# Making TensorE's 128-column products as four products on 32-column tiles, in a fused decoder layer

## The reference, cut to what matters

```python
x = x + mixer(_layernorm(x))        # projection 512 -> 2576, causal conv of 4 taps, silu, scan over 512 tokens,
                                    # 16 heads x 16 states; y -> 1024 channels, gated by silu(z), -> 512
x = x + attention(_layernorm(x), ctx, ctx)   # q is the normed x (32 heads of 16), k = v = ctx (8 kv heads)
x = x + moe(_layernorm(x))          # 16 experts, top 2, plus a shared expert; F = 256

scores  = jnp.einsum('bkgsd,bktd->bkgst', qh, kh) / 4.0      # 512 x 512 for each of 32 heads, each batch
weights = jax.nn.softmax(scores, axis=-1)
out     = jnp.einsum('bkgst,bktd->bkgsd', weights, vh)
```

## Time and profile before

| | |
|---|---|
| median of 3 runs | 1274.8 us (1274.4 to 1276.44) |
| the profiled execution | 1273.91 us |
| its span, first to last instruction | 1272.1 us |
| mean granted TensorE clock | 0.988 of 2.4 GHz |
| PE busy | 1212.4 us (95% of the span), 5041 matmul records |
| PEld / DVE / ACT / POOL busy | 40% / 53% / 38% / 25% |
| attention slot 0 begins | 191.4 us |

### The profile page before, as it was taken

How to read it: one execution, slowest core, us unless ns; L and a number is a source line. 1 busy time by engine, 2 the same in 40 slices (tenths; PEclk the granted TensorE clock), 3 DMA queues, 4 the chain that set the end, 5 groups by cost and what they waited for, 6 DMA issues and landing times. The chain is left out here.

```text
span 1272.1 us, 14831 instructions
## 1 busy us (share of the span) xinstructions
PE 1212.4 (95%) x5041; PEld 508.7 (40%) x5046; DVE 673.8 (53%) x1116; ACT 486.2 (38%) x685; POOL 314.8 (25%) x459
## 2 busy tenths in 40 slices
PE   6999999999999999999999999999988999999995
PEld 3444434343434434344433333333334444444442
DVE  3833595656687565668574776767447222222220
ACT  3311324534555353555453455555520222222221
POOL 6012310311321220221032121111103344444443
PEclk9989999999999999999999999999998999999998
DMA  8320774104374101263500255000037465678640
GB/s 197 98 76 21 202 145 111 34 5 113 83 144 84 55 22 37 72 134 80 106 9 14 87 97 76 35 2 1 34 120 273 89 171 109 163 214 226 165 88 17
DMA packets 112963, 121.14 MB, mean 95 GB/s; under 512 B 18897, under 2 KB 78417, under 8 KB 112769
## 3 DMA queue, kind: packets, MB, share of 16 engines
q1 hardware_dynamic: 101936, 99.11, 30.1%
q0 software_dynamic: 10528, 21.12, 8.4%
q10 hardware_dynamic: 432, 0.08, 0.0%
HBM read 94.63 MB, written 28.97 MB: 97 GB/s over the span
## 5 line engine op out<-in xcount | busy, mean ns | idle before, releaser
L670 DVE TENSOR_REDUCE mx<-ps_m 128x2 f32<-128x1024 f32 x256 | 313.2, 1223 | 244.1 <-PE ps_m L1141 242.1
L839 ACT ACTIVATE prob<-ps_s 128x1024 f32<-128x1024 f32 x256 | 261.9, 1023 | 335.2 <-PE ps_s L1124 335.2
L1066 PE MATMUL acc<-xnT,wring 128*128 128x512 f32 x560 | 279.8, 599 | 2.8 <-DVE xz L588 2.0
L1773 PE MATMUL ps_gu<-ring,xgT 128*128 x376 | 176.7, 593 | 0.9 <-issue 0.9
L1141 PE MATMUL ps_m<-k_stack,q_stack 96*128 96x512 bf16 x512 | 153.0, 380 | 6.6 <-DVE mx L670 5.9
L1124 PE MATMUL ps_s<-q_stack,k_stack 99*128 99x512 bf16 x512 | 153.9, 382 | 5.5 <-ACT prob L839 5.3
L1502 DVE COPY xgT<-ps_x 128x512 f32<-128x512 f32 x47 | 32.5, 691 | 204.5 <-PE ps_x L1745 200.0
L1154 PE MATMUL ps_o<-prob,values 128*32 128x512 f32 x1024 | 138.3, 604 | 0.0
L1066 PEld LDWEIGHTS acc<-xnT,wring 128*128 128x128 f32 x560 | 104.5, 192 | 70.3 <-issue 36.8
L1453 POOL DMA_INDIRECT out<-y,dest x47 | 74.4, 1584 | 156.3 <-DMA out<-y,dest 105.8
L1124 PEld LDWEIGHTS ps_s<-q_stack,k_stack 99*128 99x128 bf16 x512 | 35.5, 97 | 183.2 <-issue 131.6
(11 more groups left out here) (271 smaller groups left out, 1203.5 us busy)
## 6 DMA issues: line engine op xcount, KB each, us to landing
ring<-in_w_experts SPq DMA_DIRECT2D x96, 256.0 KB
wring<-in_w_in SPq DMA_DIRECT2D x80, 256.0 KB, 3.6
q_stack<-part_rows SPq DMA_DIRECT2D x96, 128.0 KB, 4.8
wring<-in_w_out SPq DMA_DIRECT2D x32, 256.0 KB, 3.0
part_rows<-part SPq DMA_DIRECT2D x20, 384.0 KB, 3.8
xt<-in_x SPq DMA_DIRECT2D x16, 256.0 KB, 4.1
k_stack<-part_rows SPq DMA_DIRECT2D x48, 64.0 KB, 4.2
xn_rows<-xt SPq DMA_DIRECT2D x3, 1024.0 KB, 4.2
```

The source lines that it names most:

```text
L670: nc.vector.tensor_reduce(mx[:, n % G, 2 * u:2 * u + 2], ps_m[:, :, :], AX.X, ALU.max).then_inc(s_max, 1)
L839: nc.scalar.activation(prob[:, slot % PROB, :, :], ps_s[:, :, :], ACT.Exp, scale=SCALE).then_inc(s_exp, 1)
L1066: ins = nc.tensor.matmul(bank(b, n), weights, xnT[:, k, :], start=(k == 0), stop=(k == KD - 1))
L1773: ins = nc.tensor.matmul(ps_gu[p][:, :], xgT[:, p, k * P:(k + 1) * P], weights(own)[:, k * 2 * F:(k + 1) * 2 * F], start=(k == 0), stop=(k ...
```

## The change

A switch `tiled[0]` is off in the slots below 0 and on from slot 0 to the end of the stream phase. While it is on, each product that went through the whole array is issued as four: the stationary operand is cut into four slices of 32 columns, each slice goes to its column tile, all four read the same moving operand, and each writes its 32 partitions of the same PSUM bank. The semaphore increment sits on the fourth. The waits stay ahead of the first.

The fp32 transposes (L978, L985, L992, L1029, L1169, L1184) stay as they were, whole-array operations. `transpose_max` (bf16, 12 columns) and the products that already were on column tiles are not edited.

```diff
             taken = []
+            tiled = [False]
+
+            def product(dst, stationary, moving, start, stop):
+
+                if not tiled[0]:
+                    return nc.tensor.matmul(dst, stationary, moving, start=start, stop=stop)
+                for c in range(0, P, 32):
+                    ins = nc.tensor.matmul(dst[c:c + 32, :], stationary[:, c:c + 32], moving, start=start, stop=stop,
+                                           tile_position=(0, c))
+                return ins
...
-                    ins = nc.tensor.matmul(ps_t[:, :], state_sum[:, k, :], csb[:, k, :],
-                                           start=(k == 0), stop=(k == NS - 1))
+                    ins = product(ps_t[:, :], state_sum[:, k, :], csb[:, k, :], start=(k == 0), stop=(k == NS - 1))
...
-                ins = nc.tensor.matmul(bank(b, n), weights, xnT[:, k, :], start=(k == 0), stop=(k == KD - 1))
+                ins = product(bank(b, n), weights, xnT[:, k, :], start=(k == 0), stop=(k == KD - 1))
...
-                    ins = nc.tensor.matmul(ps_s[:, i, :], k_stack[:, g, t * P:(t + 1) * P],
-                                           q_stack[:, g * R + r, :], start=True, stop=True)
+                    ins = product(ps_s[:, i, :], k_stack[:, g, t * P:(t + 1) * P], q_stack[:, g * R + r, :],
+                                  start=True, stop=True)
...
             for slot in span:
                 b, m = mixing(slot)
                 n, u = divmod(slot, UNITS)
+                tiled[0] = slot >= 0
```

More of the change, by code:

```diff
@@ L1080, in heads_to_inner @@
                     pe.wait_ge(s_icopy, 4 * b + i // 2)
-                nc.tensor.matmul(bank(b, H_BANK + i), wh2i[:, i * P:(i + 1) * P], y_parts[:, :],
-                                 start=True, stop=True).then_inc(s_h2i, 1)
+                product(bank(b, H_BANK + i), wh2i[:, i * P:(i + 1) * P], y_parts[:, :], start=True, stop=True
+                        ).then_inc(s_h2i, 1)
             def project_out(b, j, i):
@@ L1095, in project_out @@
                     pe.wait_ge(s_x1, TB * b + j - 1)
-                ins = nc.tensor.matmul(bank(b, OUT_BANK + j), gated[i][:, j * P:(j + 1) * P], ring[:, w % RING, :],
-                                       start=(i == 0), stop=(i == KI - 1))
+                ins = product(bank(b, OUT_BANK + j), gated[i][:, j * P:(j + 1) * P], ring[:, w % RING, :],
+                              start=(i == 0), stop=(i == KI - 1))
                 if i == KI - 1:
@@ L1140, in max_scores @@
                     r, t = u // 2, 2 * (u % 2) + i
-                    ins = nc.tensor.matmul(ps_m[:, i, :], q_stack[0:KQ, g * R + r, t * P:(t + 1) * P],
-                                           k_stack[0:KQ, g, :], start=True, stop=True)
+                    ins = product(ps_m[:, i, :], q_stack[0:KQ, g * R + r, t * P:(t + 1) * P], k_stack[0:KQ, g, :],
+                                  start=True, stop=True)
                 ins.then_inc(s_mm, 1)
@@ L1197, in front @@
                         col = k * 2 * F + part * F + f * P
-                        ins = nc.tensor.matmul(acc[part], w_shared[:, col:col + P], xnT[:, k, :],
-                                               start=(k == 0), stop=(k == KD - 1))
+                        ins = product(acc[part], w_shared[:, col:col + P], xnT[:, k, :],
+                                      start=(k == 0), stop=(k == KD - 1))
                         if k == KD - 1:
@@ L1210, in front @@
                             pe.wait_ge(s_fadd, TB * a + j - 1)
-                        ins = nc.tensor.matmul(acc[j % 2], th[:, f, j * P:(j + 1) * P],
-                                               w_shared[:, WUP + f * D:WUP + (f + 1) * D], start=(f == 0), stop=(f == 1))
+                        ins = product(acc[j % 2], th[:, f, j * P:(j + 1) * P],
+                                      w_shared[:, WUP + f * D:WUP + (f + 1) * D], start=(f == 0), stop=(f == 1))
                         if f:
```

## The result

The changed kernel takes 1264.18 us (median of 4 runs, 1262.82 to 1267.14) against 1275.12 us for the kernel before; the ratio is 0.9919, 95% interval 0.9905 to 0.9934. That is 10.9 us less; 8.3 less (1266.5) was forecast. The profiled execution is the slowest of the four, 1267.14 us with a span of 1265.3.

The account below looks back on a forecast made before the run. PE, streaming without gaps except at changes of tile width, was taken to bound the attention stage. -32.6 + 20.3 + 4.0 = -8.3 us, from 1273.9 to 1265.6, or 1266.5 against the median of the runs; range 1257 to 1273.

Parts of the forecast that it names:

- Removed, 0.24 us a trip: From slot 0, 136 passages from whole array to 32-column tiles and back disappear, 0.24 us each, 32.6 us saved.
- Added, 0.29 us for each of 70 transposition blocks: From slot 0, wide fp32 transposes among narrow products cost two width changes and exposed loads, 20.3 us in all.
- The products themselves, nothing: About 1720 wide matmul records become four narrow ones each, streaming as fast as one wide; nothing added to the sum.
- Rivals 4 and 5: Slower: narrow loads not hidden, at most 0.025 us a record, 0.07; four bf16 streams below one stream's rate, 1486, 0.05.
- Waits, 4 us: PE gives back 2.7 us at the row maximum after 720 us and 1.5 us in the mixer's chain, together 4.
- The place that I named: After 720 us, successive `max_scores` cannot start closer than 1.92 us; 15 halves of pairs give back 0.18 each, 2.7 us.
- Rival 3, no change: The saving is waited away: VectorE or ScalarE takes up another 6 us, time 1272.5 to 1277; chance 0.07.

Follow-up runs that it names:

- The two kernels with more changes: The changed kernel with column tiles of 64 in place of 32, 1292.25 us, and with only its fp32 products narrow, 1324.17 us.

## Why the prediction was right

*Removed, 0.24 us a trip.* Right. The three terms as printed add up to 0.23; finer starts give 0.240 for the typical block (0.092 before it, 0.141 in it, 0.007 behind it). In the changed kernel the block takes 0.86 in place of 0.99, the 0.09 before it is gone, and a pair of slots takes 6.04 us (from the scores at 602.72 to those at 608.76) in place of 6.27. The two kernels with more changes give 0.10 to 0.13 us a change by division. One group costs more than the forecast had: the 31 blocks with 12-column transposes before them. With wide neighbours such a block takes 1.18 us (239.51 to 240.69 in the kernel before), with narrow ones 1.00:

```profile
240.69 0.61 PE L1124 MATMUL ps_s<-q_stack,k_stack 99*128 99x512 bf16 x2
```

```profile
595.69 0.33 PE L1009 MATMUL ps_t<-identb,mpart 128*12 128x128 bf16 x3
...
596.69 0.68 PE L974 MATMUL ps_s<-q_stack,k_stack 99*32 99x512 bf16 x8
```

With the 0.09 and 0.01 around it that is 0.28 a trip, 1.2 us more for the 31.

*Added, 0.29 us for each of 70 transposition blocks.* Right, term by term. The way out is 0.116 (0.12 forecast), the exposed wide load with the way back in 0.150 (0.06 + 0.09), and the exposed narrow load 0.023 (0.02). What the forecast lacked is the lag of one tile: in 12 of the stage's 69 blocks the way out takes 0.18, 0.06 more, 0.7 us in all.

*The products themselves, nothing.* Right, and this was the step without a row for bf16 at 512 columns. Rivals 4 and 5 are refuted by the timeline after: 0.215 a bf16 set, 0.43 an fp32 set, loads 0.43 us ahead. By the rule in the Trainium skill, "TensorE: Matmul & The Clock Gate", section Part 3, that a load overlaps a matmul in flight only in another row group, column tiles would show their loads, since they share their row group. That does not hold here. The typical set between narrow neighbours is within 0.003 us of its wide price, and the 0.02 us of an exposed load is found behind a transposition. The same Part of the Trainium skill also names the background weight buffer as a way for a load past a matmul in flight; that would fit both this and the hidden loads of the wide kernel, but no run here tells which way it is.

*The drain.* The Trainium skill, "TensorEngine Tiling (Array Packing)", section Key Properties, gives the drain without a figure. The runs add the figure, 0.10 to 0.13 us a change with the loads that it exposes, and that tiles of 64 and of 32 are two modes in this sense.

*Waits, 4 us.* About right, a little too dear. With these prices the stage's 134 trips cost 103 x 0.24 + 31 x 0.28 = 33.4 us before and its 69 blocks 69 x 0.29 + 0.7 = 20.7 us after, so 12.7 us should have gone. 9.4 went, and 3.3 are given back. Slots 0 to 164 gave back 1.0 of 9.4 us (529.9 to 521.5 us, 86 trips against 39 blocks), the slots behind them 2.2 of 3.2 (204.3 to 203.4 us, 48 against 30); the forecast had 1.5 and 2.7. These are differences of large products of small prices, so a digit more would claim too much. The place that I named shows how it happens. Timeline of PE after 720 us in the changed kernel, as in the earlier trace rows:

```profile
779.26 0.61 PE L974 MATMUL ps_m<-k_stack,q_stack 96*32 96x512 bf16 x8
779.70 1.03 PE L1163 MATMUL ps_o<-prob,values 128*32 128x512 f32 x8
780.56 0.60 PE L974 MATMUL ps_s<-q_stack,k_stack 99*32 99x512 bf16 x8
781.21 0.62 PE L974 MATMUL ps_m<-k_stack,q_stack 96*32 96x512 bf16 x8
```

The block is 0.86 and the distance of the two maxima is 1.95 us, where it was 1.97: the scores' own step, 780.56 to 781.21, grew from 0.44 to 0.65. Of 0.24 saved, 0.02 is kept in this pair. In the mixer's slots the view of waits has 10.7 us in all, where it had 9.7. The same slots have to be compared, 191.4 to 721.3 us before and 194.2 to 715.7 us after, because the first two slots behind them have long waits of their own. The largest of after:

```profile
PE ps_m L974 <- DVE mx L670: 2.7, 5, 0.9
PE acc L974 <- DVE xz L606: 2.2, 3, 0.7
PE ps_s L974 <- ACT prob L839: 1.7, 6, 0.3
PE ps_t L974 <- DVE ao L739: 1.4, 3, 0.5
PE acc L974 <- DVE xz L611: 1.1, 3, 0.4
```

The first two are as before (2.8 and 2.3), the exponential's fell from 2.8. The fourth, for `outputs`, was 0.7, and the last is new. So it is waits along the mixer's own chain that grew, and not that for the row maximum.

*Rival 3, no change.* Its mechanism is real and takes over two thirds of the late part's gain (2.2 of 3.2 us); it is the whole stage that it does not cover.

*The size.* In the stage 8.2 was forecast (134 x 0.24 - 69 x 0.29 - 4.0) and 9.4 measured. The 12-column blocks gave 1.2 more than forecast, the waits took 0.7 less, and the lag took 0.7. That two of these cancel is luck. The median of the launch moved by 10.9; the 1.5 us between is within the scatter of the parts at its ends.

## What to carry to other kernels

On TensorE a change of tile width between neighbouring instructions costs about a tenth of a microsecond and exposes the next weight load. Where a stream that keeps the array full mixes narrow and wide products, count the changes, and make neighbours alike rather than each product as wide as it can be: four 32-column tiles with one moving operand cost no more than the whole array (here for moving operands of 512 columns, bf16 and fp32). Then decide the width for stretches, not for all: work that is dearer in narrow form (four fp32 transposes, 0.44 us wide and 0.88 as narrow products) is best left among wide products.

## What the runs showed of the hardware that was not expected

- A column tile runs on by itself. The 12-column transposes occupy one tile alone: three products of the next block start before the last of them, the product on that tile 0.1 us behind the first (595.81 and 595.91 us). Its tile then stays 0.07 us behind the other three through many products, which is why records of eight last 0.68 us in the timeline above in place of 0.62. It costs nothing while the stream stays narrow. A change of width waits for the last tile, and then costs 0.06 us more.
- The order of issue is not the order of start, then. The semaphore increment sits on the fourth tile's product. In the block at 595.81 us that one starts its second pass at 596.27 and the lagging tile at 596.34, so what the increment releases can be released some 0.07 us before that tile is through. Whether anything depends on it was not tested.
- The attention stage repeats to a tenth of a microsecond from execution to execution and chip to chip (734.2 to 734.3 in three profiled executions, 720.1 in two, 724.9 in two). The one exception, 1.3 us, is a stretch of 3.4 us at the lower clock. The start of slot 0 meanwhile wanders from 190.7 to 197.0 us. A stage is measured far better by its own landmarks than by the launch.
- Run-time checks of the loaded table values cost 28 us in the experts phase. Most of it is seven waits of some 3 us, one a lap of six tiles; some is time at the lower clock.
